# Attention and feed-forward on one core: who multiplies the block outputs, and how the first pair's values reach SBUF

## The reference

```python
q, k, v = x @ Wq, *split(context @ Wkv)              # per head: 64 columns
k = concatenate([null_k, k]);  v = concatenate([null_v, v])   # 1602 keys
sim = einsum('bhid,bhjd->bhij', q * s, k * s)
attn = softmax(sim)                                   # exp and a division by the sum
out = einsum('bhij,bhjd->bhid', attn, v)
out = layer_norm(out.reshape(b, -1, 1024) @ Wout, g_out)
# x + out, layer norm, three dense layers with weights of +1 and -1 and two relus, added to x
```

## Time and profile before

| | |
|---|---|
| runs before | 1304.69, 1302.45, 1304.74 us, median 1304.69 |
| profiled execution | 1302.49 us, span 1300.6 us |
| busy in the span | TensorE 1265.4 (97%), VectorE 835.9 (64%), ScalarE 918.9 (71%), GpSimd 943.7 (73%) |
| head, to the first scores of pair 0 | 0 to 84.9 us |
| eight pairs | 84.9 to 1063 us |
| feed-forward part | 1063 to 1300.6 us |
| mean granted clock of TensorE | 0.996 |

### The profile page before, as it was taken

The page is one execution under the profiler, slowest core; times in us unless marked ns, Lnnn a source line. Parts: engine busy times, 40 slices in busy tenths (PEclk is TensorE's granted clock), DMA queues, the critical chain, the costliest instruction groups (busy, mean ns, idle before and its releaser), DMA issues.

```text
span 1300.6 us, 20583 instructions
## 1 busy us (share of the span) xinstructions
PE 1265.4 (97%) x7342; PEld 689.6 (53%) x7342; DVE 835.9 (64%) x1220; ACT 918.9 (71%) x1182; POOL 943.7 (73%) x479
## 2 busy tenths in 40 slices
PE   6979999999999999999999999999999989999998
PEld 4534444444444444444444444444444548787876
DVE  7475767666766767676667676666775675453532
ACT  5446878888888888898888788888888662414242
POOL 0017899999999999999999999999999831010100
PEclk9999999999999999999999999999999999999999
DMA  6340111111211121112102111211432210210000
GB/s 175 114 126 31 30 38 50 52 34 34 84 34 41 37 65 34 34 41 68 34 34 68 44 40 34 75 34 34 126 107 87 66 53 9 97 65 17 1 17 16
DMA packets 59806, 70.84 MB, mean 54 GB/s; under 512 B 14336, under 2 KB 42043, under 8 KB 59707
## 3 DMA queue, kind: packets, MB, share of 16 engines
q1 hardware_dynamic: 53851, 64.43, 15.9%
q10 hardware_dynamic: 5856, 5.11, 1.3%
HBM read 51.83 MB, written 17.69 MB: 53 GB/s over the span
## 4 chain that ended last, share of the span: by engine, by line
PE 91%; DVE 4%; ACT 2%; DMA 2%; issue 1%; SPq 0%; DVEq 0%; ACTq 0%
PE ps_ox L1610 29%; PE ps_s L1597 22%; PE ps_ox L1463 10%; PE ps_ox L1713 8%; PE ps_s L1713 5%; PE ps_ox L1523 4%; PE ps_s L1685 3%; PE ps_ox L1514 2%; PE ps_ox L1512 2%; PE ps_ox L1545 1%; PE ps_ox L1468 1%; PE ps_ox L1480 1%; DMA v_scratch<-vsb 1%; DVE ps_s L1289 1%; DVE acc_d L1199 1%
## 5 line engine op out<-in xcount | busy, mean ns | idle before, releaser
L993 ACT ACTIVATE prob<-ps_s,keybias 128x1024 f32<-128x1024 f32 x416 | 441.3, 1111 | 119.6 <-PE ps_s L1597 119.0
L1610 PE MATMUL ps_ox<-prob,vp 128*64 128x512 f32 x1664 | 404.7, 607 | 4.8 <-DMA vp<-v_scratch 4.8
L1167 DVE TENSOR_REDUCE mxh<-ps_ox 128x2 f32<-128x1024 f32 x249 | 305.2, 1226 | 153.5 <-PE ps_ox L1463 149.6
L761 POOL TENSOR_TENSOR acc<-acc,prob 128x1024 f32<-128x1024 f32 x163 | 390.1, 2393 | 16.5 <-ACT prob L993 14.6
L973 ACT ACTIVATE ps_s<-shift 128x512 f32<-128x512 f32 (+1 forms) x400 | 309.3, 814 | 0.0
L761 POOL TENSOR_TENSOR acc_odd<-acc_odd,prob 128x1024 f32<-128x1024 f32 x120 | 286.4, 2386 | 5.2 <-ACT prob L993 5.2
L1610 PEld LDWEIGHTS ps_ox<-prob,vp 128*64 128x64 f32 x1664 | 101.2, 136 | 194.4 <-issue 142.7
L1597 PE MATMUL ps_s<-qh,kh 64*128 64x512 f32 x832 | 174.4, 413 | 4.0 <-DVE ps_s L1289 3.2
L1463 PE MATMUL ps_ox<-kh,qh 64*128 64x512 f32 x756 | 173.7, 452 | 2.8 <-DVE mxh L1167 2.7
L1289 DVE COPY ps_s<-shift 128x512 f32<-128x512 f32 (+1 forms) x216 | 155.5, 723 | 18.4 <-ACT prob L993 18.3
L1597 PE MATMUL ps_s<-ql,kh 64*128 64x512 f32 x832 | 166.4, 392 | 0.0
(11 more groups left out here) (180 smaller groups left out, 1425.7 us busy)
## 6 DMA issues: line engine op xcount, KB each, us to landing
shift<-m_scratch SPq DMA_DIRECT2D x32, 512.0 KB, 3.7
rb<-r_scratch SPq DMA_DIRECT2D x64, 128.0 KB, 3.0
o_scratch<-o_sb SPq DMA_DIRECT2D x32, 256.0 KB, 2.0
otb<-o_scratch SPq DMA_DIRECT2D x4, 2048.0 KB, 7.8
vp<-v_scratch SPq DMA_DIRECT2D x8, 832.0 KB, 5.1
v_scratch<-vsb SPq DMA_DIRECT2D x12, 512.0 KB, 3.2
xs<-in_x SPq DMA_DIRECT2D x4, 512.0 KB, 6.7
xres<-in_x ACTq DMA_DIRECT2D x1, 2048.0 KB, 10.2
```

What stands on the lines that cost most here:

```text
L761: gp.tensor_tensor(sum_to, terms[0], terms[1], ALU.add).then_inc(sums_p, 1)
L993: act.activation(prob[:, slot(u, s), :, :], ps_s[s % S_BUFS][:, :, :], ACT.Exp, bias=keybias[:, kt:kt + 1], scale=SCALE).then_inc(p_made, 1)
L1167: dve.reduce_max(mxh[:, :, i // MXF, i % MXF], ps[:, :, 0:MXW], AX.X).then_inc(x_free, 1)
L1610: last = pe.matmul(ps_o[qb % 2][rows(g), :], vp[u][:, kt, rows(g)], prob[:, slot(u, s), g, :], start=(kt == 0), stop=(kt == KT - 1))
```

## The change

1. The multiply of a block's output by the reciprocals moves from GpSimd to VectorE for the 30 blocks where it was GpSimd's. On VectorE it stands at the end of the cycles `NORM_AT` = 13, 19, 0, 6 (blocks 0 and 1 in their own pair, 2 and 3 in the next), behind the seed and the inversion of that cycle. `normalise_late` goes, and its two places call the new `normalise_o`. The reciprocals' cycles (`RECIP_AT` = 11, 17, 24, 4) stay.
2. In the head, GpSimd copies the pair-0 columns of each evicted values tile from `vsb` into `vp[0]`, each after the eviction of that tile's first half. ScalarE, before it overwrites a buffer of `vsb`, waits for the copy too. SyncE writes the null row over them with a transfer of its own, behind the issue of the last store and before its waits for the stores, and the 832 KB load of `vp[0]` goes.

```diff
+NORM_AT = (13, 19, 0, 6)
...
+        vp0_filled = sem("vp0_filled")
...
+            sp.wait_ge(vp0_filled, KT)
+            sp.dma_start(vp[0][NULL_ROW:NULL_ROW + 1, NULL_TILE, :].rearrange("a (h d) -> a h d", h=2),
+                         null_kv[1:2, :].unsqueeze(1).broadcast_to([1, 2, HD])).then_inc(v_loaded[0], 16)
             for r in range(2):
                 sp.wait_ge(v_stored[r], 16 * ((KT + 1 - r) // 2))
             sp.wait_ge(v_rest, 16)
             sp.wait_ge(v_null, 32)
-            sp.dma_start(vp[0][:, :, :], v_dram[0]).then_inc(v_loaded[0], 16)
...
-            def normalise_o(n, qb):
-
-                b = blocks(n, qb)
-                gp.wait_ge(r_loaded, 32 * (b + 1))
-                gp.wait_ge(o_copied, b + 1)
-                gp.tensor_tensor(o_sb[qb % 2][:, :], o_sb[qb % 2][:, :], rb[:, :], ALU.mult).then_inc(norm_done, 1)
-
...
                         add(n, u, qb, k)
-                        if qb == 0 and k == 0 and not first:
-                            normalise_o(n - 1, 2)
-                    if qb == 0 and not first:
-                        normalise_o(n - 1, 3)
-                    if qb:
-                        if qb < 3:
-                            normalise_o(n, qb - 1)
             gp.sem_inc(sums_p, 1)
             gp.wait_ge(init, 6)
+            for kt in range(KT):
+                gp.wait_ge(vh_free, 2 * kt + 1)
+                gp.tensor_copy(vp[0][:, kt, :], vsb[kt % 2][:, 0:P]).then_inc(vp0_filled, 1)
             pair_loop(gp, body)
...
                 if half == 0 and kt >= 2:
                     act.wait_ge(v_stored[kt % 2], 16 * (kt // 2))
+                    act.wait_ge(vp0_filled, kt - 1)
...
-            def normalise_late(qb):
-
-                b = blocks(PAIRS - 1, qb)
+            def normalise_o(n, qb):
+
+                b = blocks(n, qb)
                 dve.wait_ge(r_loaded, 32 * (b + 1))
                 dve.wait_ge(o_copied, b + 1)
-                dve.wait_ge(norm_done, b)
                 dve.tensor_tensor(o_sb[qb % 2][:, :], o_sb[qb % 2][:, :], rb[:, :], ALU.mult).then_inc(norm_done, 1)
...
                             invert(n - 1 if qb == 3 else n, qb, first and qb == 0)
+                    for qb in range(QB):
+                        if NORM_AT[qb] == c and not (first and qb >= 2):
+                            normalise_o(n - 1 if qb >= 2 else n, qb)
...
                     if start and j == 1:
-                        normalise_late(2)
+                        normalise_o(PAIRS - 1, 2)
                     if start and j == 7:
-                        normalise_late(3)
+                        normalise_o(PAIRS - 1, 3)
```

## The result

The kernel after took 1313.66 us (median of four runs, 1313.02 to 1316.66), the kernel before 1304.72 beside it (1302.45 to 1304.81): a ratio of 1.0079, with an interval of 1.0065 to 1.0093. That is 9 us slower by the medians, 10 by the ratio. The forecast was 1313. The profiled execution of after is the longest of its four, 1316.66 us with a span of 1314.7; its three other spans were 1311.1 to 1311.9.

The account below looks back on a forecast made before the run. TensorE was taken to set the pace, with GpSimd keeping up with nearly nothing to spare. 1302.5 - 7.2 (first pair's values) + 17.9 (multiplies on VectorE) = 1313.2, forecast 1313 us, range 1296 to 1322.

Parts of the forecast that it names:

- What bounds the kernel: In whole pairs TensorE sets the pace, busy 120.98 of 121.00 us; relieving GpSimd gains nothing.
- Part 1, the wait: At the first pair's start, the first value product starts at 92.2 instead of 96.65: 4.45 us gained.
- its two ends for the null row: Head's end: the row lands by 87 on its own, or about 92.2 behind the last store; 92.2 was taken.
- Part 1, the clock: Behind the first value product, 5.65 us busy at the lower clock would run at full: 2.8 us gained.
- Part 2, blocks 0 and 2: Multiplies at cycles 13 and 0 wait for GpSimd's add: stalls of 1.25 us in 7 pairs, 0.76 in 6.
- Blocks 1 and 3: Multiplies at cycles 19 and 6: stalls of 0 and 0.1 us, the latter 0.6 us over 6 pairs.
- The last pair: Block 26 stalls 2.95 us through late reciprocals and an add, block 27 1.0, blocks 28 and 29 0.
- rival (b): Longer stalls make the clock fall: 1316 from the 2.95 us stall, 1328 if also at seven 1.25 stalls; chance 0.12.
- The sum: Whole kernel: 1302.5 - 7.2 + 17.9 = 1313.2 us; against the median of before, 1315.4.
- (a): In the pairs, VectorE's multiplies slip between GpSimd's adds and cost almost nothing: 1296.9 us; chance 0.22.
- (c): The start gains nothing, as copies or null row come as late as the load: 1320.4 us; chance 0.06.
- (d): Every moved multiply meets an add that has just started, costing 43.8 us: 1339.1 us; chance 0.05.

Follow-up runs that it names:

- with the null row ahead: Kernel after, with the null row's transfer issued between the two halves of the last tile's store instead of behind both: 1313.80 us, ratio 1.0075.
- part 1 alone: Kernel before plus only the on-chip copies and the null row's own transfer, multiplies staying with GpSimd: 1297.27 us, ratio 0.9956.
- cycle 14: Kernel after with block 0's multiply one cycle later, NORM_AT 14 in place of 13: 1307.50 us, ratio 1.0029.
- the one-input run: Kernel after with each of the 30 moved multiplies replaced by a one-input reduction over one element of the same 128x512 tile: 1297.10 us, ratio 0.9956.
- Part 2 alone: Kernel after without the on-chip copies, so VectorE multiplies and the first pair's values come by the load as before: 1320.98 us, ratio 1.0134.
- the narrow multiply: Kernel after with each of the 30 moved multiplies cut to 64 of its 512 columns: 1306.42 us, ratio 1.0019.
- part 1 with the null row ahead: Kernel before plus the on-chip copies, with the null row's transfer ahead of the 62-row store and multiplies on GpSimd: 1296.50 us, ratio 0.9942.

## Why the prediction was right, step by step

**What bounds the kernel.** Right, but for two places. GpSimd is busy for 920.6 in place of 943.7 us, and whole pairs are not shorter for it: with GpSimd relieved and VectorE's added instruction made harmless, TensorE is busy for 120.99 of 121 us, as in the earlier trace rows. But I put GpSimd's relief at nothing, and it gave 0.3 us near 869 and 0.6 near 1010. The second is this wait of TensorE in before (first line), gone in after (second):

```profile
1009.82 3.48 PE L1480 MATMUL ps_ox<-wo_sb,otb 128*128 128x256 f32 x15 [0.56 <-issue]
...
1022.31 3.50 PE L1476 MATMUL ps_ox<-wo_sb,otb 128*128 128x256 f32 x15
```

In before the load of `otb`, which needs block 28's multiplied output, lands at 1009.73; in after, where VectorE makes this multiply 3.4 us earlier against TensorE's work, it lands at 1020.88, 1.4 us ahead of the product. A gap at this place (0.18 to 0.56 us) stands in the five profiles of kernels in which GpSimd multiplies and in none of the nine others; so it is with a gap of 0.36 us near 869, of which I have not followed the cause.

**Part 1, the wait.** I gave 4.45 us, from 96.65 to 92.2. The product started at 92.56, 4.1 earlier; the head itself ran 0.4 later in that execution, so the step holds. In after's two later profiles it started at 93.61 and 93.14 without any wait, for the clock fell earlier there and slowed the work ahead of it; before's three profiles have a wait of 3.40 to 5.68 us at this place. Of its two ends for the null row the later one was right (chain of after: its transfer stood from 83.93, for 8.58 us), and that it would sit behind the last store was right. Not foreseen was that SyncE itself stands there for 5.71 us, up to 89.64. It cost nothing: its next issue waits for the stores, and came 9.3 us behind the store's first half in after (83.16 and 92.47) and 9.4 with the null row ahead (82.57 and 91.99).

**Part 1, the clock.** This is the term that was mis-sized. I took the second stretch of the earlier trace rows as the consequence of the 4.77 us of idleness, counted its 2.8 us as gained, and gave no granted clock of 0.50 from 95 on as a sign of being right. But after has its own stretch of 6.83 us in the head's end in each of three profiles (in the first it lasts to 97.41), and so has part 1 alone. Over all profiles the head's end has 10.24 or 13.65 us at 0.50 in the four with the load, and 6.83 in eight and 10.24 in two of the ten without it: less, but never none. The gaps of 1.52 and 1.39 us ahead of the value product stay, and where the clock falls after them varies. The lateness behind the head's end was -4.4, -5.6 and -6.1 us in after's three profiles and 0, +0.3 and -0.7 in before's three, all against before's first: 5.2 us of gain on average, and 5.7 over all fourteen profiles, so that, with 4.45 for the wait, the clock gave about 0.8 to 1.3 in place of 2.8. By the timed runs part 1 alone gained 5.7 us by its ratio, with an interval of 3.9 to 7.4, which does not exclude my 7.2.

**Part 2, blocks 0 and 2.** Right, and to within a tenth: 1.25 predicted, 1.22 to 1.28 measured, seven times (8.7 and 8.8 us); 0.76 predicted, 0.78 to 0.82 measured, six times (4.6 and 4.8), of which about 0.1 comes back each time. The working that did it was the end of the running add plus 0.54 us, less the slack of TensorE; and that the adds kept their phase, the point on which I had least to go, held in every pair. One cycle later it would have been a matter of hundredths of a us, as cycle 14 showed. The multiplies average 1.78 us, just under the 1.8 to 2.2 that I gave as a sign. The one-input run shows the cause and not the effect alone.

**Blocks 1 and 3.** 0 and 0.1 predicted, 0 measured in both.

**The last pair.** Block 26: 2.95 predicted, gaps of 2.67, 2.71 and 2.38 in the three profiles of after. Block 27, for which I took 1.0 without knowing the phase: 0.3. Left out of the forecast was the clock: 3.41 us at 0.50 behind block 26, 1.7 us lost, in all three. That is rival (b), with its place and its smaller size; at the stalls of 1.2 us in the pairs the clock did not fall, so its larger form didn't come. The -0.6 us near 1010 is the wait for `otb` above.

**The sum.** Part 2 was 17.9 in the prediction; in the first trace of after the terms without the clock make 15.1, and with its 1.7 us, 16.8. Part 2 alone cost 17.5 us by its ratio (15.5 to 19.4). Part 1 was 7.2 and came out between 4.4 and 6.1 in the profiles. The forecast of 1313 against a median of 1313.66 rests on misses of both signs: in part 2 the clock behind block 26 was left out (1.7 too little) and the rest was 2.8 too much, and in part 1 the clock's term was 1.5 to 2 us too much. A part of the closeness is luck of another kind: the sum starts from 1302.5, which is near the fastest of before's runs. From before's median the same terms give 1315.4, 1.7 over what was measured. As a difference, 10.7 was forecast and 8.9 (medians) to 10.3 us (ratio) came.

**The rivals.** (a), that VectorE slips between the adds, is out for blocks 0 and 2 at the places of the change: the multiplies wait in each pair. At cycle 14 it came in four pairs of seven. What it gave for the time, 1296.9, is near what the one-input kernel took (1297.10), where nothing waits. (c) is out by part 1 alone. (d), a fresh add each time, came up at cycle 14, with 2.80 to 2.92 us for three multiplies, and cost 0.5 to 0.6 us each, for that place has more slack behind it. What a fresh add would cost at the four places of the change, the 43.8 us of the upper bound, no run showed.

## What to carry to other kernels

Before an elementwise instruction with two SBUF inputs goes to VectorE, look at what GpSimd does at that moment: in this kernel the price was the rest of the running add plus 0.54 us, where the one-input form cost nothing. Work such a move out place by place, as the end of the other engine's instruction plus the tail, less the slack of the engine that sets the pace; the place with the longest instruction need not be the one with the longest stall. Where the place lies at the seam between two of those instructions, hundredths of a us decide which engine waits, and it can differ from one pass of the loop to the next. And of a change with two parts run each alone, for the good one (here 0.9956, and 0.9942 with the null row ahead) can hide behind the bad one.

## What the runs showed of the hardware

A multiply never waited for more than one add: it took 0.68 to 2.51 us in after's three profiles and part 2 alone, and up to 2.92 where the add had just begun. Which of the two waits went by the order of their starts: at cycle 14 an add that began 0.03 to 0.11 us ahead of the multiply made it 2.80 to 2.92 us long, and one that began with it or up to 0.03 us later left it at 0.68 and was itself 2.89 to 2.93 long. GpSimd's next add is recorded as starting 0.59 us before the multiply's end (522.87 and 523.46) and takes 2.81 in place of 2.39 us, so that it in turn waits for most of what is left of the multiply.

A transfer of two rows issued right behind one of 62 rows held SyncE's issue for 5.68 to 5.71 us in eight profiles, and for 0.64 and 0.65 in the two where it was issued ahead of it. The Trainium skill (DMA: Bandwidth & Descriptors, section "Queues, rings and completion order") gives each pair of a queue and an engine a ring of its own, and the two transfers share a queue; whether a full ring is what held SyncE, no row here shows.

The granted clock fell to 0.50, the lower level (1.2 GHz), for 3.41 to 10.24 us at a time, but not after every gap of one size. Behind the gap of 2.2 to 2.7 us in the last pair it fell in six of seven profiles (three of after, part 2 alone, the narrow multiply and cycle 14; not with the null row ahead, at 2.52 us). Behind the gap of 1.95 us near 1042 (1054 in after), which stands in all fourteen profiles, it fell in five: one of three of after, two of three of before, the narrow multiply's and that of part 1 with the null row ahead. Behind the gaps of 1.0 us in the pairs it never fell. One profile of a kernel therefore leaves some 2 to 3 us open here.
